# Four attentions of a decoder: exponentials of turned scores, and sequences half a step apart

## Chip, cores and metric

The kernel runs on one core of one Trainium2 chip. The metric is the device time in microseconds (us) of that core; lower is better.

## The reference

A decoder over 16 sequences of 128 tokens, width 128, 16 heads of 8. Fifteen stages follow each other; after each sub-layer `x = layernorm(x + sublayer(x))`. Four of them are attentions of this form, with softmax over the keys in float32:

```python
def attention(x, c, Wq, bq, Wk, bk, Wv, bv, Wo, bo, mask):
    qh, kh, vh = split_heads(x @ Wq + bq), split_heads(c @ Wk + bk), split_heads(c @ Wv + bv)
    s = einsum('bhqd,bhkd->bhqk', qh, kh) / sqrt(8)
    attn = softmax(s + mask, axis=-1)
    return merge_heads(einsum('bhqk,bhkd->bhqd', attn, vh)) @ Wo + bo
```

- X0 (`S_X0`): queries from x, keys and values from a context; keys masked per sequence.
- SELF2 (`S_SELF2`): q, k and v come from MLPs, computed for all sequences by the stage before and kept in SBUF; no mask.
- X2 (`S_X2`): like X0, without a mask.
- MQA (`S_MQA`): q and k are rotated by position; causal mask.

The others are an LSTM with positional attention, an attention with a threshold (REG), a linear attention (LIN), a wide one-head attention, feed-forward layers, a latent attention (LAT) and a mixture of experts.

## The kernel before

Everything stays in SBUF: `x_all` holds the state, a stage reads and writes it sequence by sequence. Each engine has its own hand-written program, and semaphores couple them. There are two buffers, `arena[0]` and `arena[1]`, and two sets of four PSUM banks, `ps[0]` and `ps[1]`; a loop turn works on a pair of sequences, s = 0 and 1, one in each (`pairs`, `PAIRS` = 8). The attention functions `att_pe`, `att_act`, `att_dve` and `att_pool` serve the four stages above and REG and LIN. Phase by phase, for both sequences of a pair:

1. POOL copies x (and the context) to the arena; PE transposes x and makes q, k (turned: width on partitions) and v, with bias products (L496 to L504, in PSUM banks 3 and 2); ACT copies them out (L623, L626), in MQA DVE rotates q and k instead (L692, L695). In SELF2 ACT copies the kept q and v.
2. POOL widens k (L422): 128x512, in which each of four column groups keeps only one head of each row group. PE then gets the scores of four heads with one fp32 product of 32 rows and 512 columns (L521), four of them for 16 heads, each into its bank, in the order 1, 2, 3, 0. Masks are added by a bf16 product with the identity (L535). Queries lie on the partitions, keys along the free axis.
3. DVE takes the maximum of each head (L727). For banks 1 and 3 it only scales the maximum (L730) and ACT exponentiates four heads separately with it as bias (L643); for banks 2 and 0 DVE subtracts (L733) and ACT exponentiates 512 columns (L640).
4. PE transposes the weights, 16 of 128x128 (L557), back into the score banks, ACT copies them out (L648), and PE multiplies values by turned weights (L543; the values carry a column of ones, which gives the sum). ACT copies the result (L653), PE turns it back (L571), DVE divides by the sum (L747, L754).
5. PE transposes the result (L580), ACT copies it (L661), PE multiplies by the output weights (L587); DVE adds x and takes mean and variance (L380, L338, L340, L343), POOL takes the power -1/2 (L332), DVE normalises (L347).

In the loop body the projections of the next pair are issued before phase 5, and widening k of its second sequence stands behind the norm's power on POOL. Tile names: `ps` is PSUM, `C` the constants (`ident` is the identity), `WA` and `WB` weights, `R` rows of gains and biases. The profile gives the line of the helper, L314 for a bias product (`add_bias`), L332 to L347 for the norm. An fp32 product is two MATMUL records with two LDWEIGHTS, a transpose or a bf16 product one. The latent stage, to which the prediction refers, is another function: there DVE scales maxima (L2044) while POOL scales weights (L1827).

## Time and profile before

| | us |
|---|---|
| median of 3 runs | 2589.38 (2586.69 to 2591.61) |
| profiled execution | 2588.07 |
| its span | 2586.3 |

| engine | busy us | share | instructions |
|---|---|---|---|
| PE, matmul | 1804.1 | 70% | 13203 |
| PE, weight load | 1172.2 | 45% | 13225 |
| DVE (VectorE) | 1442.6 | 56% | 4308 |
| ACT (ScalarE) | 1170.4 | 45% | 3283 |
| POOL (GpSimd) | 583.3 | 23% | 910 |

The profiled execution took 2588.07 us, of which the span of the records is 2586.3. The four attentions lie at 310 to 483 us (X0), 1165 to 1322 (SELF2), 1322 to 1500 (X2) and 1697 to 1881 (MQA). The mean granted TensorE clock is 0.877 of full speed over the span. The ends of matmuls in the records are modelled, so PE's busy share is no share of its peak. The profile slices the span in 40 parts of 64.7 us.

### The profile page before, as it was taken

The page shows a single profiled execution, that of the slowest core. Times are in us where ns is not written, and L with a number is a line of the kernel's source. Part 1 is how long each engine was busy: PE and PEld are TensorE (multiplying, and loading weights), DVE is VectorE, ACT ScalarE, POOL GpSimd, SP SyncE. Part 2 cuts the span into 40 slices and gives each one's busy share as a digit, 9 for nine tenths or more (in the row PEclk, how much of TensorE's full clock was granted, in tenths as well). Part 3 has the DMA queues.
Part 4 walks back from the last instruction along what each step waited for, and adds up shares of the span by engine and source line. Part 5 has one row for each costly group of instructions (what it writes and reads, how often), then busy time and mean ns, then how long its engine had stood idle before and what let it go on. Part 6 is the DMA issues. An engine that isn't in the chain of part 4 may idle for free.

```text
span 2586.3 us, 43908 instructions
## 1 busy us (share of the span) xinstructions
PE 1804.1 (70%) x13203; PEld 1172.2 (45%) x13225; DVE 1442.6 (56%) x4308; ACT 1170.4 (45%) x3283; POOL 583.3 (23%) x910
## 2 busy tenths in 40 slices
PE   2444488677755565797778821178878999998798
PEld 1333244344433353454445410144466777776343
DVE  3322555556667656316655567756655444453677
ACT  1222466456611132237756621146646655555343
POOL 2500411111122232101111133321133333333110
PEclk9999999799967687798888855589989999999899
DMA  5000000000000000000020000000000000000000
GB/s 179 1 0 0 0 0 0 0 1 0 0 1 0 0 0 0 0 0 0 0 84 0 0 1 0 0 1 0 0 1 0 0 0 0 0 0 1 1 0 16
DMA packets 2924, 18.74 MB, mean 7 GB/s; under 512 B 1073, under 2 KB 1201, under 8 KB 1585
## 3 DMA queue, kind: packets, MB, share of 16 engines
q1 hardware_dynamic: 2866, 18.02, 1.9%
q8 instruction: 30, 0.49, 0.1%
q14 instruction: 28, 0.23, 0.0%
HBM read 16.90 MB, written 1.05 MB: 7 GB/s over the span
## 4 chain that ended last, share of the span: by engine, by line
issue 53%; PE 18%; POOL 13%; POOLq 5%; ACT 5%; DVE 4%; DVEq 2%; ACTq 0%
POOL arena L1827 5%; PE ps L2195 4%; POOL arena L332 4%; POOL arena L422 3%; PE ps L521 3%; PE ps L1722 2%; ACT arena L648 1%; PE ps L535 1%; DVEq L728 1%; PE ps L314 1%; PE ps L1733 1%; ACT arena L643 1%; ACT arena L640 1%; POOLq L1515 1%; POOL arena L1499 1%
## 5 line engine op out<-in xcount | busy, mean ns | idle before, releaser
L332 POOL TENSOR_TENSOR arena<-arena,C 128x1 f32<-128x1 f32 (+1 forms) x272 | 158.0, 583 | 741.8 <-DVE arena L343 736.8
L557 PE MATMUL ps<-C,arena 128*128 128x128 f32 x1280 | 212.5, 306 | 76.6 <-ACT arena L643 64.2
L643 ACT ACTIVATE arena<-ps,arena 128x128 f32<-128x128 f32 x640 | 186.5, 394 | 172.2 <-DVE arena L730 172.2
L521 PE MATMUL ps<-arena 32*128 32x512 f32 x768 | 164.7, 769 | 108.1 <-POOL arena L422 107.4
L422 POOL TENSOR_TENSOR arena<-arena,C 128x512 f32<-128x512 f32 x96 | 99.9, 1041 | 602.3 <-ACT arena L623 303.4
L727 DVE TENSOR_REDUCE arena<-ps 128x4 f32<-128x512 f32 x320 | 219.2, 685 | 20.1 <-PE ps L535 10.0
L557 PEld LDWEIGHTS ps<-C,arena 128*128 128x128 f32 x1280 | 148.5, 152 | 160.6 <-ACT arena L643 123.9
L1827 POOL TENSOR_TENSOR arena<-arena 128x512 f32<-128x512 f32 x128 | 133.7, 1045 | 248.9 <-DVE arena L2050 245.7
L648 ACT COPY arena<-ps 128x512 f32<-128x512 f32 x320 | 166.5, 643 | 0.0
L543 PE MATMUL ps<-arena 128*32 128x128 f32 x3072 | 154.6, 305 | 7.9 <-DVE arena L717 0.9
L1055 PE MATMUL ps<-hid,WA 128*20 128x16 f32 x1024 | 57.3, 197 | 119.2 <-DVE hid L1115 114.3
L1978 ACT ACTIVATE arena<-ps,arena 128x256 f32<-128x256 f32 x256 | 119.3, 471 | 33.5 <-DVE arena L2044 21.4
L2195 PE MATMUL ps<-WA,arena 128*128 128x512 f32 x256 | 132.7, 600 | 0.9 <-ACT arena L2219 0.4
L521 PEld LDWEIGHTS ps<-arena 32*128 32x128 f32 x768 | 50.3, 214 | 170.2 <-issue 141.6
L1894 PE MATMUL ps<-arena 128*128 128x256 f32 x512 | 120.2, 386 | 0.2
L347 DVE TENSOR_SCALAR x_all<-arena 128x128 f32 x192 | 96.8, 504 | 41.4 <-POOL arena L332 40.9
L733 DVE TENSOR_TENSOR arena<-ps,arena 128x512 f32<-128x512 f32 x160 | 110.7, 692 | 12.9 <-issue 1.5
L2042 DVE TENSOR_REDUCE arena<-ps 128x2 f32<-128x512 f32 x128 | 87.7, 685 | 51.5 <-PE ps L1894 51.5
L380 DVE TENSOR_TENSOR arena<-ps,x_all 128x128 f32<-128x128 f32 x112 | 32.6, 291 | 150.2 <-PE ps L314 79.8
L1531 PE MATMUL ps<-C,arena 128*128 128x128 f32 x32 | 13.1, 461 | 147.7 <-DVE arena L1624 108.1
L640 ACT ACTIVATE arena<-arena 128x512 f32<-128x512 f32 x160 | 106.4, 665 | 19.9 <-DVE arena L733 19.9
L1904 PE MATMUL ps<-C,arena 128*128 128x128 f32 x512 | 86.2, 310 | 41.5 <-POOL arena L1827 40.9
(364 smaller groups left out, 4048.1 us busy)
## 6 DMA issues: line engine op xcount, KB each, us to landing
WA<-w_late SPq DMA_DIRECT2D x1, 4228.0 KB, 13.1
R<-rows SPq DMA_DIRECT2D x1, 2114.0 KB, 10.8
WA<-w_early SPq DMA_DIRECT2D x1, 1600.0 KB, 24.9
WB<-w_rest SPq DMA_DIRECT2D x1, 1152.0 KB, 18.2
xT_all<-x_T SPq DMA_DIRECT2D x1, 1024.0 KB, 6.2
...
```

What stands on the lines that cost most here:

```text
L332: nc.gpsimd.tensor_tensor(v_(s, cols, "rstd", 0, n), v_(s, cols, "mv", 1, 2 * n - 1)[:, ::2] if n > 1 else v_(s, cols, "mv", 1, 1), cst("m ...
L422: return eng.tensor_tensor(heads(v_(s, ATT, "wide", 0, 512)), src.unsqueeze(1).broadcast_to([128, 4, 128]), cst("tilemask").unsqueeze(2).b ...
L521: mm = nc.tensor.matmul(ps[s][t][:, :], v_(s, ATT, "kT" if kind == "linear" else "qT")[rows, :], v_(s, ATT, "wide", 0, 512)[rows, :], star ...
L543: mm = nc.tensor.matmul(ps[s][1][PAD * j:PAD * (j + 1), t * 128:(t + 1) * 128], va[:, 4 * t + j, :], v_(s, ATT, "PT", 128 * (4 * t + j), 128),
L557: mm = nc.tensor.transpose(ps[s][t][:, j * 128:(j + 1) * 128], v_(s, ATT, "P", 128 * (4 * t + j), 128), ident)
L640: nc.scalar.activation(e, e, ACT.Exp, scale=SCALE).then_inc(p_exp, 1)
L643: ex = nc.scalar.activation(e[:, 128 * j:128 * j + 128], ps[s][t][:, 128 * j:128 * j + 128], ACT.Exp, scale=SCALE, bias=v_(s, ATT, "m", 4 ...
L648: nc.scalar.copy(v_(s, ATT, "PT", 512 * t, 512), ps[s][t][:, :]).then_inc(pT_sb, 1)
L727: nc.vector.tensor_reduce(m[:, 4 * t:4 * t + 4], heads(ps[s][t][:, :]), AXX, ALU.max)
L1827: nc.gpsimd.tensor_tensor(p, p, rec.unsqueeze(2).broadcast_to([128, 2, 256]), ALU.mult).then_inc(l_sub, 1)
L1894: mm = nc.tensor.matmul(ps[s][t][:, 256 * (h % 2):256 * (h % 2) + 256], v_(s, LAT, "qT", 128 * h, 128), kT[:, 4 * hf + t, :], start=True, ...
L2195: nc.tensor.matmul(o, v_(s, MOE, "xT"), WA[:, W_LATE("experts", FF * e, FF)], start=True, stop=False, skip_group_check=True)
```

## The change

X0, SELF2, X2 and MQA get functions of their own (`satt_pool`, `satt_pe`, `satt_act`, `satt_dve`); REG and LIN keep the old ones. Two things change.

**Turned scores.** The scores are computed twice. The first time as before, with masks, for the maxima of each query (`scores`, `maxima`). The second time turned, keys on partitions and queries along the free axis: the widened operand is now q, the other k (`scores_T`), and masks are added turned (`mask_T`). A maximum belongs to a query, which is now a column, so it can't be a bias. DVE cuts the 16 maxima of each query into a bf16 part and a bf16 rest (`m_cols`), PE transposes them by a product with the identity, DVE multiplies them with a mask of -1 into a bf16 operand (`FOLD`), and PE adds this with a product with ones (`fold_T`). ACT then exponentiates 512 columns four times out of PSUM straight into the place of turned weights. The transposes of the weights and their copies are gone. POOL widens k and q.

**Half a step apart.** A turn of the loop still holds two sequences, but as two steps, one after the other (`in_turn`, `step`). In the step of sequence n, PE also issues the scores of n+1, the projections of n+2 and the output product of n-1; DVE also takes the maxima of n+1 and the norm of n-1.

Core of the diff (call sites, semaphores and declarations left out; `z` is the other buffer):

```diff
+        WIDE_Q, OT, FOLD, TURN = 0, 512, 1024, 1280
+
+        T_ORDER = (2, 3, 0, 1)
+        def satt_pool(pool, sub, kind):
...
+            def wides(i, s, d):
+                pool.wait_ge(qk_sb, nth(a, i, s + d))
+                if sub == S_X0:
+                    nc.gpsimd.tensor_copy(m_mask[s][:, :], x_at(maskadd, i, s + d)).then_inc(mask_sb, 1)
+                widen(nc.gpsimd, s, "wide", "kT").then_inc(k_wide, 1)
+                widen(nc.gpsimd, s, "P", "qT").then_inc(q_wide, 1)
+            def step(i, s, before=True, after=True, ahead=True):
+                if ahead:
+                    stage(i, s, 2)
+                if before:
+                    finish(i, s)
+                if ahead:
+                    wides(i, s, 2)
...
+        def satt_pe(pe, sub, kind, W, name, bias_name, mask_kind, out_w=384, out_name=None):
...
+            def scores_T(s, t):
+                nc.tensor.matmul(ps[s][t][:, :], v_(s, ATT, "kT")[rows(t), :],
+                                 v_(s, ATT, "P", WIDE_Q, 512)[rows(t), :], start=True, stop=False,
+                                 skip_group_check=True)
+            def fold_T(s, t, stop):
+                fold = v_(s, ATT, "P", FOLD, 256).bitcast(BF16)
+                return nc.tensor.matmul(ps[s][t][:, :], ones_b[rows(t), :], fold[rows(t), :], start=False, stop=stop,
+                                        skip_group_check=True)
+            def step(i, s, before=True, after=True, ahead=True):
+                pe.wait_ge(s_max, nth(st, i, s))
+                pe.wait_ge(q_wide, nth(st, i, s))
+                for t in T_ORDER[0:3]:
+                    scores_T(s, t)
+                if before:
+                    turned(i, s)
+                pe.wait_ge(m_cut, nth(st, i, s))
+                nc.tensor.matmul(ps[s][1][:, 0:128], m_cols[s][:, :], ident_b[:, :], start=True,
+                                 stop=True, skip_group_check=True).then_inc(mT_ps, 1)
+                if mask_kind is not None:
+                    for t in T_ORDER[0:3]:
+                        mask_T(s, t, False)
+                if before:
+                    output(i, s)
+                pe.wait_ge(m_fold, nth(st, i, s))
+                for t in T_ORDER[0:3]:
+                    fold_T(s, t, True).then_inc(sT_ps, 1)
+                scores_T(s, 1)
+                mm = fold_T(s, 1, mask_kind is None)
+                if mask_kind is not None:
+                    mm = mask_T(s, 1, True)
+                mm.then_inc(sT_ps, 1)
+                if after:
+                    scores(i, s, 1)
...
+                for n, t in enumerate(T_ORDER):
+                    pe.wait_ge(pT_sb, nth(a, i, s, GROUPS, n + 1))
...
+                mm.then_inc(oT_ps, 1)
+                if ahead:
+                    front_x(i, s, 2)
+                pe.wait_ge(oT_sb, nth(a, i, s))
...
+                mm.then_inc(o_ps, 1)
+                if ahead:
+                    front_qkv(i, s, 2)
...
+        def satt_act(act, sub, kind):
...
+            def step(i, s, before=True, after=True, ahead=True):
+                if before:
+                    turned(i, s)
+                for n, t in enumerate(T_ORDER):
+                    act.wait_ge(sT_ps, nth(st, i, s, GROUPS, n + 1))
+                    nc.scalar.activation(v_(s, ATT, "PT", 512 * t, 512), ps[s][t][:, :], ACT.Exp,
+                                         scale=SCALE).then_inc(pT_sb, 1)
+                act.wait_ge(oT_ps, nth(a, i, s))
+                nc.scalar.copy(v_(s, ATT, "P", OT, 512), ps[s][2][:, :]).then_inc(oT_sb, 1)
+                if ahead:
+                    front_x(i, s, 2)
+                    front_qkv(i, s, 2)
...
+        def satt_dve(dve, sub, kind):
...
+            def step(i, s, before=True, after=True, ahead=True):
+                m = heads(v_(s, ATT, "m"))
+                cut = m_cols[s][:, :].rearrange("p (t c) -> p t c", c=PAD)
+                dve.drain()
+                nc.vector.tensor_copy(cut[:, :, 0:4], m)
+                dve.drain()
+                nc.vector.tensor_tensor(cut[:, :, 4:8], m, cut[:, :, 0:4], ALU.subtract).then_inc(m_cut, 1)
+                dve.wait_ge(mT_ps, nth(st, i, s))
+                nc.vector.tensor_tensor(heads(v_(s, ATT, "P", FOLD, 256).bitcast(BF16)),
+                                        ps[s][1][:, 0:128].unsqueeze(1).broadcast_to([128, 4, 128]),
+                                        cst("foldmask").unsqueeze(2).broadcast_to([128, 4, 128]),
+                                        ALU.mult).then_inc(m_fold, 1)
+                if before:
+                    moments(i, s)
+                if after:
+                    maxima(i, s, 1, 0, 2)
+                if before:
+                    normed(i, s)
+                if after:
+                    maxima(i, s, 1, 2, 4)
+                dve.wait_ge(o_ps, nth(a, i, s))
...
+                if ahead and sub == S_MQA:
+                    rope(i, s, 2)
```

How the order moves on PE in X2, in the last pair, which has no next one. Before, with the scores of both sequences ahead of it (`ps0` and `ps1` are the banks of the two sequences, L521 scores, L557 transposes of weights, L543 values, L571 turning back):

```order
L557 MATMUL ps0_1<-C,arena0 128x128 x4
L557 MATMUL ps0_2<-C,arena0 128x128 x4
L557 MATMUL ps0_3<-C,arena0 128x128 x4
L557 MATMUL ps0_0<-C,arena0 128x128 x4
L543 MATMUL ps0_1<-arena0 32x128 x16
L557 MATMUL ps1_1<-C,arena1 128x128 x4
L557 MATMUL ps1_2<-C,arena1 128x128 x4
L557 MATMUL ps1_3<-C,arena1 128x128 x4
L557 MATMUL ps1_0<-C,arena1 128x128 x4
L543 MATMUL ps1_1<-arena1 32x128 x16
L571 MATMUL ps0_0<-C,arena0 128x128 x4
L571 MATMUL ps1_0<-C,arena1 128x128 x4
```

Now, in one step of the loop, sequence 1 (L913 turned scores, L931 the result of sequence 0, L950 the maxima, L937 and L326 the output of sequence 0, L925 folds, L900 scores of the next sequence, L973 values):

```order
L913 MATMUL ps1_2<-arena1 128x512
L913 MATMUL ps1_3<-arena1 128x512
L913 MATMUL ps1_0<-arena1 128x512
L931 MATMUL ps0_2<-C,arena0 128x128
L950 MATMUL ps1_1<-ident_b,m_cols1 128x128
L937 MATMUL ps0_3<-WB,arena0 128x128
L326 MATMUL ps0_3<-bias3,ones_b 128x128
L925 MATMUL ps1_2<-arena1,ones_b 128x512
L925 MATMUL ps1_3<-arena1,ones_b 128x512
L925 MATMUL ps1_0<-arena1,ones_b 128x512
L913 MATMUL ps1_1<-arena1 128x512
L925 MATMUL ps1_1<-arena1,ones_b 128x512
```

```order
L900 MATMUL ps0_1<-arena0 128x512
L900 MATMUL ps0_2<-arena0 128x512
L900 MATMUL ps0_3<-arena0 128x512
L900 MATMUL ps0_0<-arena0 128x512
L973 MATMUL ps1_2<-arena1 32x128 x16
L867 MATMUL ps1_0<-C,arena1 128x128
L981 MATMUL ps1_3<-C,arena1 128x128 x4
```

The scores of the next sequence now stand between the last turned product and the values, and the output product of the sequence before stands ahead of the folds.

DVE in MQA, before, at the end of a pair (L747 and L754 divide by the sums, L692 and L695 rotate):

```order
L747 RECIPROCAL arena0<-ps0_0 128x16
L754 TENSOR_TENSOR arena0<-ps0_0,arena0 128x128
L739 REGISTER_ALU
L747 RECIPROCAL arena1<-ps1_0 128x16
L754 TENSOR_TENSOR arena1<-ps1_0,arena1 128x128
L689 ISA
L692 TENSOR_TENSOR arena0<-ps0_3,C 128x256 x2
L695 TENSOR_TENSOR arena0<-arena0 128x256
L689 REGISTER_ALU
L692 TENSOR_TENSOR arena1<-ps1_3,C 128x256 x2
L695 TENSOR_TENSOR arena1<-arena1 128x256
```

Now, at the end of the step of sequence 0 and the begin of that of 1 (L1102 and L1104 divide, L1052 and L1055 rotate, L1083 and L1085 cut the maxima, L1087 folds, L1070 begins the norm of the sequence before, L1062 takes maxima):

```order
L1102 RECIPROCAL arena0<-ps0_3 128x16
L1104 TENSOR_TENSOR arena0<-ps0_3,arena0 128x128
L1052 TENSOR_TENSOR arena0<-ps0_1,C 128x256 x2
L1055 TENSOR_TENSOR arena0<-arena0 128x256
L1083 CAST m_cols1<-arena1 128x4x4
L1085 TENSOR_TENSOR m_cols1<-arena1,m_cols1 128x4x4
L1087 TENSOR_TENSOR arena1<-ps1_1,C 128x512
L1070 TENSOR_TENSOR arena0<-ps0_3,x_all 128x128
L350 BN_STATS arena0<-arena0 128x6
L352 BN_AGGR arena0<-arena0 128x2
L355 TENSOR_SCALAR arena0<-arena0 128x1
L1062 TENSOR_REDUCE arena0<-ps0_1 128x4
```

The rotation of the sequence two further on now stands ahead of cutting the maxima of the next.

POOL in SELF2, in the loop now (L435 widens k, then q; L344 is the power of the norm):

```order
L343 ISA
L344 TENSOR_TENSOR arena1<-arena1,C 128x1
L836 REGISTER_ALU
L435 TENSOR_TENSOR arena0<-arena0,C 128x512 x2
L343 REGISTER_ALU
L344 TENSOR_TENSOR arena0<-arena0,C 128x1
L836 REGISTER_ALU
L435 TENSOR_TENSOR arena1<-arena1,C 128x512 x2
L811 REGISTER_ALU
L811 COMPARE_AND_BRANCH
```

Each step now has two widenings in one go, where it had one.

## Rows read from the trace of the kernel before

**Rows 1.** Windows: stretch, length, busy PE, PEld, DVE, ACT, POOL, clock, DMA.

```profile
310.00:483.00 173.00, 143.93 (x1247) 81.97 (x1247) 99.30 (x240) 108.34 (x304) 32.77 (x62) 0.99 0.00 0
...
329.84:478.33 148.49, 124.65 (x1091) 70.38 (x1090) 87.61 (x211) 94.05 (x264) 28.28 (x52) 0.99 0.00 0
...
1180.29:1317.19 136.90, 108.71 (x899) 61.56 (x897) 88.06 (x211) 97.81 (x256) 22.11 (x28) 0.86 0.00 0
...
1342.79:1492.44 149.65, 121.79 (x1035) 74.92 (x1034) 87.61 (x210) 94.05 (x264) 28.28 (x52) 0.87 0.00 0
...
1717.74:1875.74 158.00, 132.44 (x1175) 79.05 (x1174) 104.13 (x253) 97.09 (x256) 25.44 (x40) 1.00 0.00 0
```

**Rows 2.** Timeline, one pair of X2: start, length, engine, line, idle before.

```profile
1436.15 1.23 PE L521 MATMUL ps<-arena 32*128 32x512 f32 x8 [1.97 <-POOL arena L422]
...
1438.17 2.00 PE L557 MATMUL ps<-C,arena 128*128 128x128 f32 x8 [0.79 <-ACT arena L643]
...
1449.55 0.26 DVE L747 RECIPROCAL arena<-ps 128x16 f32<-128x16 f32 x1 [4.50 <-PE ps L571]
...
1449.88 0.29 DVE L754 TENSOR_TENSOR arena<-ps,arena 128x128 f32<-128x128 f32 x1
```

**Rows 3.** The page, granted TensorE clock in 40 slices, tenths of full.

```profile
PEclk9999999799967687798888855589989999999899
```

**Rows 4.** Groups by line and form: busy us, mean ns of one, idle before.

```profile
L727 DVE TENSOR_REDUCE arena<-ps 128x4 f32<-128x512 f32 x320 | 219.2, 685 | 20.1 <-PE ps L535 10.0 <-PE ps L521 9.6 <-issue 0.3
...
L557 PE MATMUL ps<-C,arena 128*128 128x128 f32 x1280 | 212.5, 306 | 76.6 <-ACT arena L643 64.2 <-ACT arena L640 11.5
...
L733 DVE TENSOR_TENSOR arena<-ps,arena 128x512 f32<-128x512 f32 x160 | 110.7, 692 | 12.9 <-issue 1.5
...
L640 ACT ACTIVATE arena<-arena 128x512 f32<-128x512 f32 x160 | 106.4, 665 | 19.9 <-DVE arena L733 19.9
...
L422 POOL TENSOR_TENSOR arena<-arena,C 128x512 f32<-128x512 f32 x96 | 99.9, 1041 | 602.3 <-ACT arena L623 303.4 <-DVE arena L695 102.6 <-PE ps L571 95.6
...
L535 PE MATMUL ps<-causal_b,ident_b 128*128 128x512 bf16 x64 | 16.6, 382 | 0.0
```

**Rows 5.** Timeline, where work runs back to back, in SELF2, X2 and MQA.

```profile
1269.48 2.03 ACT L648 COPY arena<-ps 128x512 f32<-128x512 f32 x4
...
1270.54 1.45 PE L543 MATMUL ps<-arena 128*32 128x128 f32 x32
...
1428.54 0.39 PE L496 MATMUL ps<-arena,WB 128*128 128x128 f32 x2
...
1429.49 0.44 PE L496 MATMUL ps<-arena,WB 128*128 128x128 f32 x2
...
1448.91 1.16 PE L571 MATMUL ps<-C,arena 128*128 128x128 f32 x8
...
1811.28 0.75 DVE L692 TENSOR_TENSOR arena<-ps,C 128x256 f32<-128x256 f32 x2 [0.41 <-PE ps L499]
...
1812.11 0.43 DVE L695 TENSOR_TENSOR arena<-arena 128x256 f32<-128x256 f32 x1
...
1816.98 1.23 PE L521 MATMUL ps<-arena 32*128 32x512 f32 x8 [0.90 <-POOL arena L422]
...
1818.14 1.04 PE L535 MATMUL ps<-causal_b,ident_b 128*128 128x512 bf16 x4
```

**Rows 6.** Timeline, small DVE operations and POOL, X2, then the latent stage.

```profile
1434.26 0.34 DVE L347 TENSOR_SCALAR x_all<-arena 128x128 f32 x1
...
1435.04 1.05 DVE L347 TENSOR_SCALAR x_all<-arena 128x128 f32 x1 [0.44 <-POOL arena L332]
...
2099.99 1.04 POOL L1827 TENSOR_TENSOR arena<-arena 128x512 f32<-128x512 f32 x1 [0.17 <-DVE arena L2050]
...
2100.61 0.45 DVE L2044 TENSOR_SCALAR arena<-arena 128x2 f32<-128x2 f32 x1
...
2101.72 0.17 DVE L2044 TENSOR_SCALAR arena<-arena 128x2 f32<-128x2 f32 x1
```

More of the change, by code:

```diff
@@ L450, in wide @@
                     pool.wait_ge(o_ps, nth(a, i, s))
-                widen(nc.gpsimd, i, d, s, kind).then_inc(wide_ok, 1)
+                widen(nc.gpsimd, s, "wide", "qT" if kind == "linear" else "kT").then_inc(wide_ok, 1)
             def body(i, ahead):
@@ L792, in att_dve, with in_turn, stage, finish @@
             pairs(dve, front, body)
+        def in_turn(eng, step, last):
+            step(0, 0, before=False)
+            step(0, 1)
+            with eng.Fori(1, PAIRS - 1) as i:
+                step(i, 0)
+                step(i, 1)
+            step(PAIRS - 1, 0, ahead=False)
+            step(PAIRS - 1, 1, ahead=False, after=False)
+            last(PAIRS - 1, 2)
+        def satt_pool(pool, sub, kind):
+            a, st = att_run[sub], st_run[sub]
+            def stage(i, s, d):
+                if d == 0:
+                    pool.wait_ge(seq_done, nth(sub, i, s))
+                elif kind == "cross":
+                    pool.wait_ge(qkv_ps, nth(qkv_run[sub], i, s, 2, 2))
+                elif kind == "self":
+                    pool.wait_ge(xT_ps, nth(xt_run[sub], i, s))
+                if kind == "cross":
+                    nc.gpsimd.tensor_copy(v_(s, ATT, "c"), x_at(ctxT_all, i, s + d))
+                if kind != "kept":
+                    nc.gpsimd.tensor_copy(v_(s, ATT, "x"), x_at(x_all, i, s + d))
+                    pool.drain()
+                pool.sem_inc(staged, 1)
+            def wides(i, s, d):
[4 more added lines that the diff above has]
+                widen(nc.gpsimd, s, "P", "qT").then_inc(q_wide, 1)
+            def finish(i, s):
+                rstd(pool, var_ok, rstd_ok, tail_run[sub], i, (s + 1) % 2, ATT, 1, s - 1 - (s + 1) % 2)
+            def step(i, s, before=True, after=True, ahead=True):
[5 more added lines that the diff above has]
+                    wides(i, s, 2)
+            for s in range(2):
+                stage(0, s, 0)
+            for s in range(2):
+                wides(0, s, 0)
+            in_turn(pool, step, finish)
@@ new lines, in satt_dve, with rope, maxima, moments @@
+        def satt_dve(dve, sub, kind):
+            a, st = att_run[sub], st_run[sub]
+            def rope(i, s, d):
+                dve.wait_ge(qkv_ps, nth(qkv_run[sub], i, s + d, 2, 1))
+                qk, turn = qkT_of(s), v_(s, ATT, "P", TURN, 256)
+                for dst, at, table in ((qk, 0, "cos"), (turn, 256, "sin")):
+                    nc.vector.tensor_tensor(heads(dst, 2), heads(ps[s][1][:, at:at + 256], 2),
+                                            cst(table).unsqueeze(1).broadcast_to([128, 2, 128]), ALU.mult)
+                dve.drain()
+                nc.vector.tensor_tensor(qk, qk, turn, ALU.add).then_inc(qk_sb, 1)
+            def maxima(i, s, d, of, to):
+                z = (s + d) % 2
+                for n in range(of, to):
+                    t = ORDER[n]
+                    dve.wait_ge(s_ps, nth(a, i, s + d, GROUPS, n + 1))
+                    red = nc.vector.tensor_reduce(v_(z, ATT, "m", 4 * t, 4), heads(ps[z][t][:, :]), AXX, ALU.max)
+                if to == GROUPS:
+                    red.then_inc(s_max, 1)
+            def moments(i, s):
+                z = (s + 1) % 2
+                r = v_(z, ATT, "r")
+                dve.wait_ge(y_ps, nth(tail_run[sub], i, s - 1))
+                nc.vector.tensor_tensor(r, ps[z][3][:, 0:128], x_at(x_all, i, s - 1), ALU.add).then_inc(y_read, 1)
+                dve.drain()
+                stats(dve, z, ATT, r).then_inc(var_ok, 1)
+            def normed(i, s):
+                z = (s + 1) % 2
+                dve.wait_ge(rstd_ok, nth(tail_run[sub], i, s - 1))
+                norm(dve, z, ATT, x_at(x_all, i, s - 1), v_(z, ATT, "r")).then_inc(seq_done, 1)
+            def step(i, s, before=True, after=True, ahead=True):
+                m = heads(v_(s, ATT, "m"))
+                cut = m_cols[s][:, :].rearrange("p (t c) -> p t c", c=PAD)
+                dve.drain()
+                nc.vector.tensor_copy(cut[:, :, 0:4], m)
+                dve.drain()
+                nc.vector.tensor_tensor(cut[:, :, 4:8], m, cut[:, :, 0:4], ALU.subtract).then_inc(m_cut, 1)
[13 more added lines that the diff above has]
+                dve.wait_ge(o_ps, nth(a, i, s))
+                o = ps[s][3][:, :].rearrange("p (h d) -> p h d", d=PAD)
+                rec = v_(s, ATT, "rec")
+                nc.vector.reciprocal(rec, o[:, :, HD:HD + 1].rearrange("p h d -> p (h d)"))
+                dve.drain()
+                nc.vector.tensor_tensor(v_(s, ATT, "O").rearrange("p (h d) -> p h d", d=HD), o[:, :, 0:HD],
+                                        rec.unsqueeze(2).broadcast_to([128, HEADS, HD]), ALU.mult).then_inc(o_sb, 1)
+                if ahead and sub == S_MQA:
+                    rope(i, s, 2)
+            def last(i, s):
+                moments(i, s)
+                normed(i, s)
+            if sub == S_MQA:
+                for s in range(2):
+                    rope(0, s, 0)
+            maxima(0, 0, 0, 0, 4)
+            in_turn(dve, step, last)
@@ L928, in start_dve @@
             nc.vector.memset(minus_round[:, :], -ROUND)
+            for s in range(2):
+                nc.vector.memset(m_cols[s][:, :], 0.0)
             dve.wait_ge(bias_in, 16)
```

174 lines of the change are left out of this document (148 added, 26 removed).

## Prediction

> **What bounds the kernel now.** I read the stretches first: what does a pair of sequences take in each of the four attentions? Between the first and the last pair, seven pairs take 148.49 us in X0, 136.90 in SELF2, 149.65 in X2 and 158.00 in MQA [rows 1], so a pair takes 21.21, 19.56, 21.38 and 22.57 us, and a sequence 10.61, 9.78, 10.69 and 11.29: 42.36 together, and 16 sequences of each 677.8 us. All of X0 is 173.0 us [rows 1], 3.3 more than eight pairs. No engine is full in them: in X2 PE is busy 121.8 of 149.65 us, DVE 87.6, ACT 94.1. So the order of the work bounds, not a count. The reader sees it next in the timeline of one pair of X2 [rows 2]: all engines do the same phase for both sequences, then hand over. PE stands 1.97 us before the second group of scores, for the widened keys of POOL, which stand behind the norm; DVE stands 4.50 us before the reciprocal, while ACT copies turned weights and PE multiplies; ACT waits out the maxima. The granted clock shows it too [rows 1, 3]: 0.99 in X0 and 1.00 in MQA, but 0.86 and 0.87 in SELF2 and X2, where after the wait of 1.97 us eight transposes take 2.00 us [rows 2].
>
> **What goes.** Per sequence 16 PE transposes of weights (L557), four ACT copies of them (four in 2.03 us) and 2 DVE subtractions (692 ns); eight short ACT exponentials become two wide ones [rows 4, 5]. What comes: four turned score products and four folded maxima on PE (and four more masks where there are any), a transpose of the maxima, one DVE fold, two small DVE operations, a second POOL widening. PE's total hardly moves: 212.5 us over 80 sequences [rows 4], 2.7 each, go; 2.6 come by the prices below. DVE is about even, ACT loses 2 us or more of its 6.7 (94.05 / 14). The gain is to come from the stagger: ACT's four exponentials of sequence n now lie beside PE's scores of n+1 and DVE's maxima of n+1, and the tail of n-1 in the gaps.
>
> **The new period.** One sequence per period; I follow the loop from the end of DVE's fold.
>
> *A, PE from the folds to the weights times values.* Four row-tiled fp32 score products take 1.23 us with their tail, the masks start 1.16 after them; four masks take 1.04, one alone 382 ns, so 0.22 apart and 0.16 of tail [rows 4, 5]. Three folds: side by side in separate rows 0.3, one after another 0.65; I take 0.5, and 0.2 for the last. The turned product left alone: no row shows one. At least a quarter of a group, 0.3; at most what a whole group takes, 1.16; being alone it has nothing to share its stream with, so 0.9. Next scores 1.2. Values: after ACT's last copy (1269.48 + 2.03 = 1271.51) PE ended at 1271.99 [rows 5]; less hand-over and tail a quarter is 0.25, so 1.0. Without masks 0.5 + 0.9 + 0.2 + 1.2 + 1.0 = **3.8**; with masks 0.2 and 0.9 more, **4.9**. Covered: ACT's exponentials, 0.35 + 4 x 0.55 = 2.55 (L640's 0.665 is one with its latency, the copies came 0.5 apart), against 2.8 of PE ahead of the values; DVE's norm of n-1 and its four maxima (0.685 each [rows 4]), done just before the sums are. If PE's part shrank, those maxima would set the end next.
>
> *B.* Tail, ACT's copy of the sums 0.65, two hand-overs: 0.9. Then four transposes, half of the eight in 1.16: 0.5 [rows 5]. Together **1.4**.
>
> *C, until the small maxima operations are done.* X0 and X2: PE issues the three projections of n+2, 0.95 (L496 at 1428.54 and 1429.49 [rows 5]), three turned products 0.9 and a transpose 0.15: **2.0**. DVE takes 1.3 beside it: hand-over 0.1, the product 0.33 behind the reciprocal [rows 2] and 0.29 long, cast and subtraction 0.5 with their drains (0.17 is what a 128x2 operation takes [rows 6]). SELF2 has no projections, so DVE's 1.35 would set it. MQA must rotate: DVE needs four of its five projections, 4/3 of 0.95 or 1.3, 0.2 of tail and hand-over, then 0.75 + 0.43 + 0.1 [rows 5] and 0.5 for the small ones: 3.3.
>
> Here a lock counts. In the latent stage DVE's tensor_scalar on 128x2 takes 0.17 us alone and 0.45 when POOL's tensor_tensor runs: it ends with that one, at 2101.06 against 2101.03. The norm at 1435.04 takes 1.05 instead of 0.34, under a widening [rows 6]. So even tiny operations between places in SBUF wait for POOL's running instruction. The change issues two widenings of 1.04 us [rows 4] per sequence as soon as q and k lie ready: in SELF2 while DVE does the reciprocal, so the cast or the subtraction waits for the rest of the second, +1.0; in MQA in the same instant as the cast, so the subtraction waits for the first, +0.7. In X0 and X2 q and k are ready 1.3 us after the projections begin, when both are just over: 0. Bounds: 0 and 2.1. So SELF2 **2.35**, MQA **4.0**. The Trainium skill says the same more widely ("SBUF — State Buffer", Who interferes with whom): a DVE cast, or one with two SBUF inputs, is fully blocked by a GpSimd instruction that reads SBUF. By that rule the cast and the subtraction both count, and the fold, with one input in PSUM, doesn't; the rows above agree for a tensor_scalar, and for a subtraction no row here shows it.
>
> *D.* The maxima's transpose and hand-overs 0.35, DVE's fold 0.7 (L733, 692 ns, the nearest [rows 4]) and 0.05: **1.1**. PE's output and masks (1.0) fit beside it.
>
> Sum: X0 4.9 + 1.4 + 2.0 + 1.1 = **9.4**; X2 **8.3**; SELF2 3.8 + 1.4 + 2.35 + 1.1 = **8.65**; MQA **11.4**. Together 37.75, times 16 is 604: 74 us less than 677.8. MQA gains nothing; its rotation and the small operations lie end to end. The ends cost more: before, X0 had 3.3 us beside its pairs. Now the first sequence waits for its scores and maxima alone (1.2 + 2.4) while the last steps are short; I take 3 a stage, 12 (bounds 0 and 6). ACT's table load (1.28 us a pair in SELF2 and MQA) falls between the copy of the outputs and the first exponential, where ACT waits. POOL's rstd comes before DVE has done two maxima. So 62 us less: 2588.07 (span 2586.3) becomes **2526 us**. The median of the runs, 2589.38, lies 1.3 from the profiled one.
>
> **The clock.** I take it full in all four. Before, it was low after the wait of 1.97 us in X2; MQA waits 0.90 at that place [rows 5] and keeps 1.00. The longest PE wait in the sum is SELF2's, 1.4.
>
> **Rivals.**
> 1. *No lock on the small operations.* The 128x2 operation is a tensor_scalar; a cast to bf16 of 4x4 may run free. SELF2 -1.0, MQA -0.7, times 16: -27, **2499 us**. Against it speak the 0.45 and 1.05 us [rows 6]. Chance 0.13.
> 2. *The clock stays where it was*, 0.86 in SELF2 and X2. PE paces 4.5 us of SELF2's period (A, the transposes, little else) and 6.9 of X2's (A, transposes, C, the start of D). At 0.86 to 0.87 they take 0.155 more: 11.4 x 0.155 x 16 = +28, **2554 us**. For it: both stages keep several short waits in each period. Against: the long one goes. Chance 0.17.
> 3. *The lock takes both small operations.* If POOL starts a moment ahead of the cast, the cast waits for the first widening and the subtraction for the second: +1.3 in MQA, +0.5 in SELF2, times 16: +29, **2555 us**. Chance 0.10.
> 4. *Slower: the clock falls to its lower level.* A stage with several PE waits each period can lose the full clock: the feed-forward stage behind X2 has 5 and 5 in its slices [rows 3]. Where SELF2 and X2 ran at 0.5 throughout, +182: **2708 us**. The point from which it is no gain is 182 x (1/c - 1) = 62, c = 0.75 in these two (or 0.87 in all four, where PE paces some 27 us of the 37.75). For it speak SELF2's 0.86 before and its lock; against it, that no wait is as long as before. Chance 0.05.
> 5. *The turned products do not run side by side*, 0.9 each: three are 2.7. +1.8 in X0 and X2, +0.5 in SELF2: +66, **2592 us**, no change. L521's groups of four in 1.16 us, fp32 and row-tiled alike, speak against it. Chance 0.02.
>
> My forecast has 0.53. **Range**: down to rival 1 with the lone product and folds cheaper (16 us), 2485; up to rival 2 or 3 and some 20 us of a dearer lone product or ends, 2575. Outside remain the fifth and fourth, and the tails. Faster by over 0.2% (5 us, about what a measurement here can tell from no change): 0.92. Within: 0.02. Slower: 0.06.
>
> **What would show it.** Product starts (DVE's x rec) 9.4, 8.65, 8.3, 11.4 us apart in X0, SELF2, X2, MQA. In SELF2 and MQA a cast or subtraction of 0.5 to 1.2 us that ends with a widening; in X0 and X2 at 0.2. ACT idle before the first exponential, not after. PE's longest wait for the maxima's cast in SELF2 and MQA, for ACT's copy of the sums in X0 and X2. PEclk 0.95 or more in all four. It is wrong if the periods are right but the clock isn't, if PE waits for exponentials before the values, or if a lone turned product takes 0.4 or 2 us.

## Result, and the profile after

| | before | after |
|---|---|---|
| median, us | 2589.38 | 2606.34 (2602.17 to 2608.71, 5 runs) |
| profiled execution, us | 2588.07 | 2608.71 |
| its span, us | 2586.3 | 2606.8 |
| mean granted clock | 0.877 | 0.847 |
| ratio of times | | 1.0064, interval 1.0053 to 1.0075 |

The changed kernel is slower by 0.6%; 2526 us was forecast. Busy times and the granted clock in 40 slices, from the page of the kernel after (the clock line answers to [rows 3]):

```profile
PE 1861.7 (71%) x13161; PEld 1155.5 (44%) x13161; DVE 1417.9 (54%) x4246; ACT 961.7 (37%) x2631; POOL 647.4 (25%) x990
...
PEclk9999999699967777886669755688789999998899
```

ACT lost 209 us of work and the kernel gained no time by it. PE has 42 fewer matmuls, but 57.6 us more busy time. Counted from 0, slices 18 to 20 (SELF2) and 26 to 29 (MQA) show where its clock went.

Windows of the kernel after (stretch, length, busy PE, PEld, DVE, ACT, POOL, clock, DMA), against [rows 1]: first X0 as a whole; then each stage from the start of the first sequence's product (x rec) to that of the last; then pieces of SELF2 and MQA:

```profile
310.00:471.50 161.50, 146.86 (x1265) 74.37 (x1264) 86.06 (x225) 58.99 (x144) 54.24 (x95) 0.97 0.00 1
...
328.80:465.08 136.28, 128.64 (x1159) 65.31 (x1157) 76.78 (x206) 54.31 (x131) 46.43 (x83) 1.00 0.00 0
1168.63:1319.22 150.59, 132.21 (x907) 64.02 (x904) 81.30 (x206) 51.47 (x116) 35.58 (x42) 0.64 0.00 0
1344.26:1462.20 117.94, 106.03 (x1045) 60.30 (x1043) 84.17 (x206) 54.38 (x131) 42.86 (x69) 0.99 0.00 1
1684.34:1896.05 211.71, 178.23 (x1243) 84.24 (x1241) 115.81 (x249) 50.74 (x117) 39.74 (x56) 0.81 0.00 0
1189.99:1205.27 15.28, 11.93 (x125) 6.13 (x127) 11.14 (x29) 6.84 (x16) 5.17 (x7) 1.00 0.01 1
1227.51:1262.03 34.52, 31.66 (x186) 15.08 (x186) 16.78 (x42) 10.58 (x24) 7.75 (x10) 0.50 0.00 0
1684.34:1696.28 11.94, 9.65 (x87) 5.17 (x86) 8.07 (x18) 3.35 (x8) 2.82 (x4) 1.00 0.01 1
```

Each piece holds whole sequences: two of SELF2 at 1.00 take 15.28 us, 7.64 each; three at 0.50 take 34.52, 11.51 each. One of MQA at 1.00 takes 11.94; others there take up to 16.8. X0 and X2 keep a steady period, 9.26 and 7.82 us, at full clock.

By stage, between the same operations in both traces (ACT's first copy of SELF2 at 1163.96 and 1152.00, the norm that ends it at 1322.06 and 1323.52, and so on): X0 12.0 us less, SELF2 13.4 more, X2 32.4 less, MQA 49.8 more, the rest 1.7 more; together the 20.5 us of the spans.

Timeline of the kernel after (start, length, engine, line, idle before in brackets): the fill of SELF2, a sequence of SELF2 at 1.00, one at 0.50, one of X2 at full clock, one of MQA on its way down:

```profile
1153.58 1.14 PE L900 MATMUL ps<-arena 32*128 32x512 f32 x8 [2.58 <-POOL arena L435]
...
1157.27 1.23 PE L913 MATMUL ps<-arena 32*128 32x512 f32 x3 [2.56 <-DVE arena L1062]
...
1161.00 1.57 ACT L1031 ACTIVATE arena<-ps 128x512 f32<-128x512 f32 x3 [6.59 <-PE ps L925]
...
1196.65 2.04 POOL L435 TENSOR_TENSOR arena<-arena,C 128x512 f32<-128x512 f32 x2 [2.61 <-ACT arena L1011]
...
1198.08 0.64 DVE L1083 CAST m_cols<-arena 128x16 bf16<-128x16 f32 x1 [0.16 <-issue]
...
1238.58 2.09 PE L913 MATMUL ps<-arena 32*128 32x512 f32 x6
...
1249.04 1.11 PE L981 MATMUL ps<-C,arena 128*128 128x128 f32 x4 [0.71 <-ACT arena L1034]
...
1375.74 0.66 PE L981 MATMUL ps<-C,arena 128*128 128x128 f32 x4 [0.45 <-ACT arena L1034]
...
1377.27 1.13 PE L913 MATMUL ps<-arena 32*128 32x512 f32 x6
...
1377.67 0.90 DVE L1085 TENSOR_TENSOR m_cols<-arena,m_cols 128x16 bf16<-128x16 f32 x1
...
1378.34 0.33 PE L931 MATMUL ps<-C,arena 128*128 128x128 f32 x1
...
1378.89 0.69 DVE L1087 TENSOR_TENSOR arena<-ps,C 128x512 bf16<-128x512 f32 x1 [0.32 <-PE ps L950]
...
1379.64 0.39 PE L925 MATMUL ps<-arena,ones_b 32*128 32x512 bf16 x3
...
1379.64 1.12 PE L913 MATMUL ps<-arena 32*128 32x512 f32 x2
...
1381.77 1.08 PE L973 MATMUL ps<-arena 128*32 128x128 f32 x32
...
1383.56 0.66 PE L981 MATMUL ps<-C,arena 128*128 128x128 f32 x4 [0.45 <-ACT arena L1034]
...
1740.73 2.04 POOL L435 TENSOR_TENSOR arena<-arena,C 128x512 f32<-128x512 f32 x2 [9.89 <-DVE arena L1055]
1740.74 1.06 DVE L1083 CAST m_cols<-arena 128x16 bf16<-128x16 f32 x1
...
1741.88 0.92 DVE L1085 TENSOR_TENSOR m_cols<-arena,m_cols 128x16 bf16<-128x16 f32 x1
...
1742.86 0.29 PE L950 MATMUL ps<-ident_b,m_cols 128*128 128x128 bf16 x1 [1.84 <-DVE m_cols L1085]
...
1742.93 1.49 PE L919 MATMUL ps<-ident_b,causal_b 128*128 128x512 bf16 x3
```

In MQA both widenings start with the cast; the cast ends with the first and the subtraction (0.17 us free) with the second; PE waits 1.84 us, and its masks then take 1.49 us for three, where [rows 5] has four in 1.04. In SELF2 at 0.50 PE hardly waits at all: the longest gap of the sequence at 1238 is 0.71, but six records of turned scores take 2.09 us against 1.13 at full clock. Its long waits lie ahead of the steady part, in the fill: 2.58 us before the first scores and 2.56 us before the first turned scores. There the clock falls (windows of 5 us, same columns as above):

```profile
1150.00:1155.00 5.00, 2.14 (x17) 1.08 (x16) 1.02 (x3) 2.39 (x5) 2.52 (x3) 1.00 0.01 2
1155.00:1160.00 5.00, 2.31 (x7) 0.61 (x7) 2.96 (x7) 0.00 (x0) 1.51 (x2) 0.55 0.00 0
1160.00:1165.00 5.00, 4.63 (x26) 2.15 (x30) 0.70 (x2) 2.17 (x4) 0.00 (x0) 0.50 0.00 0
```

Behind the fill it does not stay put either: the distances between SELF2's products are 11.5, 9.9, 7.6, 7.6, 10.7, four of 11.5, then 9.9, 7.6, 7.6, 10.7, 11.5 and 9.8 us, so the clock comes back twice and is lost twice, with the same work in every sequence.

Groups of the kernel after (busy us, mean ns of one | idle before), beside [rows 4]:

```profile
L913 PE MATMUL ps<-arena 32*128 32x512 f32 x512 | 177.8, 755 | 12.2 <-DVE arena L1062 12.2
...
L1062 DVE TENSOR_REDUCE arena<-ps 128x4 f32<-128x512 f32 x256 | 163.9, 685 | 153.9 <-PE ps L909 88.7 <-PE ps L900 65.2
...
L1031 ACT ACTIVATE arena<-ps 128x512 f32<-128x512 f32 x256 | 134.6, 600 | 145.0 <-PE ps L925 136.4 <-PE ps L919 8.6
```

DVE and ACT now wait for PE (the maxima 153.9 us, the exponentials 145.0); before, the maxima waited 20.1 us. PE now paces the stages, so its clock is in the time: half the clock makes 11.51 us of 7.64.

### The profile page after: what moved, and what is told of

Read it like the earlier page. It is cut to its first block, busy times and chain, and to the rows that moved or that the text cites. A ratio compares the mean times of both kernels' runs of the same rounds, so it can differ in the third digit from the quotient of the medians.

```text
span 2606.8 us, 42884 instructions
## 1 busy us (share of the span) xinstructions
PE 1861.7 (71%) x13161; PEld 1155.5 (44%) x13161; DVE 1417.9 (54%) x4246; ACT 961.7 (37%) x2631; POOL 647.4 (25%) x990
## 4 chain that ended last, share of the span: by engine, by line
issue 39%; PE 36%; POOL 10%; DVE 6%; POOLq 5%; ACT 3%; DVEq 1%; ACTq 0%
POOL arena L2156 5%; PE ps L913 5%; PE ps L2524 4%; PE ps L900 3%; POOL arena L344 3%; PE ps L973 3%; PE ps L2051 2%; PE ps L981 2%; PE ps L925 1%; PE ps L880 1%; PE ps L909 1%; PE ps L326 1%; PE ps L919 1%; PE ps L534 1%; ACT arena L1034 1%
## 5 line engine op out<-in xcount | busy, mean ns | idle before, releaser
L344 POOL TENSOR_TENSOR arena<-arena,C 128x1 f32<-128x1 f32 (+1 forms) x272 | 156.6, 578 | 768.0 <-DVE arena L355 763.0
L435 POOL TENSOR_TENSOR arena<-arena,C 128x512 f32<-128x512 f32 x160 | 163.6, 1040 | 494.0 <-ACT arena L1011 156.5
L1062 DVE TENSOR_REDUCE arena<-ps 128x4 f32<-128x512 f32 x256 | 163.9, 685 | 153.9 <-PE ps L909 88.7
L1031 ACT ACTIVATE arena<-ps 128x512 f32<-128x512 f32 x256 | 134.6, 600 | 145.0 <-PE ps L925 136.4
L913 PE MATMUL ps<-arena 32*128 32x512 f32 x512 | 177.8, 755 | 12.2 <-DVE arena L1062 12.2
L1860 PE MATMUL ps<-C,arena 128*128 128x128 f32 x32 | 13.1, 460 | 147.6 <-DVE arena L1953 107.0
L900 PE MATMUL ps<-arena 32*128 32x512 f32 x512 | 116.3, 810 | 2.6 <-POOL arena L435 2.6
L2233 PE MATMUL ps<-C,arena 128*128 128x128 f32 x512 | 86.1, 310 | 41.4 <-POOL arena L2156 40.9
L350 DVE BATCH_NORM_STATS2 arena<-arena 128x6 f32<-128x128 f32 (+1 forms) x304 | 102.0, 336 | 24.3 <-POOLq L2136 2.7
L2223 PEld LDWEIGHTS ps<-arena 128*128 128x128 f32 x512 | 94.6, 190 | 24.2 <-ACT arena L2322 6.4
L326 PE MATMUL ps<-bias,ones_b 128*128 128x128 bf16 (+1 forms) x352 | 105.3, 299 | 0.0
L534 PE MATMUL ps<-arena 32*128 32x512 f32 x256 | 52.7, 879 | 64.1 <-POOL arena L435 64.0
L359 DVE TENSOR_SCALAR x_all<-arena 128x128 f32 (+1 forms) x192 | 76.9, 401 | 34.5 <-POOL arena L344 34.0
L2233 PEld LDWEIGHTS ps<-C,arena 128*128 128x128 f32 x512 | 63.8, 156 | 62.4 <-POOL arena L2156 59.9
```

The source lines that it names most:

```text
L326: return nc.tensor.matmul(out_ap, ones_b[:, :], bias3[:, BIAS(name, of, width)], start=False, stop=stop, skip_group_check=True)
L344: nc.gpsimd.tensor_tensor(v_(s, cols, "rstd", 0, n), v_(s, cols, "mv", 1, 2 * n - 1)[:, ::2] if n > 1 else v_(s, cols, "mv", 1, 1), cst("m ...
L435: return eng.tensor_tensor(heads(v_(s, ATT, dst, of, 512)), v_(s, ATT, src).unsqueeze(1).broadcast_to([128, 4, 128]), cst("tilemask").unsq ...
L900: mm = nc.tensor.matmul(ps[z][t][:, :], v_(z, ATT, "qT")[rows(t), :], v_(z, ATT, "wide", 0, 512)[rows(t), :], start=True, stop=mask_kind i ...
L913: nc.tensor.matmul(ps[s][t][:, :], v_(s, ATT, "kT")[rows(t), :], v_(s, ATT, "P", WIDE_Q, 512)[rows(t), :], start=True, stop=False, skip_gr ...
L1031: nc.scalar.activation(v_(s, ATT, "PT", 512 * t, 512), ps[s][t][:, :], ACT.Exp, scale=SCALE).then_inc(pT_sb, 1)
```

## Experiments

The theory from the trace: the change made PE the pace of all four stages, and PE's clock fell in two of them; in MQA the lock adds its own time. Rival: the waits lower the clock, and taking the lock's wait away brings it back everywhere. In the session of the first four kernels the kernel before took 2587.03 us (7 runs), in that of the last four 2590.23 us; each ratio is to the one of its session. Below, "a sequence" is the distance between two starts of the product.

### The lock taken away: `late_widen`

```diff
                 pool.wait_ge(qk_sb, nth(a, i, s + d))
+                if d:
+                    pool.wait_ge(m_cut, nth(st, i, s + 1))
```

POOL widens for sequence n+2 only once DVE has cut the maxima of n+1.

> Edit: POOL widens k and q of sequence n+2 only after DVE has cut the maxima of n+1, so no widening can meet the cast or the subtraction. Theory 'lock wait': the 1.84 us PE wait behind cast (1.06 us) and subtraction (0.92 us) is what lets the clock fall in MQA. Then the cast and subtraction are 0.17 us everywhere, MQA's period is 10.6 to 11.2 us at a clock of 0.97 or more (234 us of stage become 180), the total about 2545 to 2560 us. Rival 'the steps themselves': the clock falls without a lock, because what remains of PE's work doesn't keep it. Then MQA gains only the 1.6 us per step it waited (about 25 us), SELF2 stays near 0.6 with periods of 11 us, total 2575 to 2585 us. SELF2 tells most: its wait for the lock is only 0.5 us.

Measured: 2543.37 us (2509.80 to 2544.93, 4 runs), ratio 0.9784 (0.9716 to 0.9852). Windows of MQA from first to last sequence, and of a piece of SELF2; then the small operations by tile (lines are 2 higher than in the kernel after; min/median/max ns):

```profile
1684.19:1835.18 150.99, 140.37 (x1243) 74.31 (x1241) 92.92 (x248) 49.62 (x117) 39.75 (x56) 1.00 0.00 1
1165.00:1280.00 115.00, 105.45 (x615) 50.21 (x614) 51.99 (x138) 35.19 (x81) 25.29 (x29) 0.50 0.00 0
```

```profile
L1085 DVE CAST m_cols<-arena x64: 174/175/176, 318.6 to 1828.9; 128x16 bf16<-128x16 f32 x64
L1087 DVE TENSOR_TENSOR m_cols<-arena,m_cols x64: 174/176/177, 318.9 to 1829.2; 128x16 bf16<-128x16 f32 x64
```

The lock is gone (longest cast 176 ns, after: 1059), and MQA takes 10.3 us a sequence at 1.00 throughout, 60.7 us less between the same points. SELF2 does not follow: nine sequences of 11.5 us, one of 9.8, and only then 7.3, 7.3, 7.3 and 8.9. So the rival holds for MQA. In SELF2 the lock's wait was not what kept the clock down: PE is 105.45 us of 115.00 busy at 0.50. The fill's waits, which this edit leaves, stand ahead of it. At full clock a sequence takes 7.3 us here against 7.6 with the lock, and X2's 7.7 against 7.8; X0 keeps 9.3. One of the four executions took 2509.8 us, with no further edit.

### Work in PE's waits: `warm_full` and `warm_rows`

```diff
+            first, second = {S_SELF2: (2, 3), S_MQA: (5, 3)}.get(sub, (0, 0))
+            def warm(o, n, k):
+                for _ in range(n):
+                    nc.tensor.matmul(heads(o, k), ident_b[slice(0, 128), :],
+                                     ones_b[slice(0, 128), :].unsqueeze(1).broadcast_to([128, k, 128]), ...)
...
+                warm(ps[s][1][:, 128:512], first, 3)
                 pe.wait_ge(m_cut, nth(st, i, s))
...
+                warm(ps[s][3][:, :], second, 4)
                 pe.wait_ge(oT_sb, nth(a, i, s))
```

The lock stays. Both kernels add idle bf16 matmuls whose results nobody reads: `warm_full` over all 128 rows of the array, `warm_rows` with `slice(0, 32)` in place of `slice(0, 128)`, over 32 rows.

> Edit: the kernel after the change, with filler products on PE in SELF2 and MQA, in the places where PE waits: before the wait for the cut maxima (2 in SELF2, 5 in MQA, 384 columns each) and before the wait for ACT's copy of the sums (3 of 512 columns). They use all 128 rows of the array, bf16, into PSUM that is free there. Both theories of the clock say that it comes back when PE has work in its waits: SELF2's clock from 0.63 to 0.9 or more, its periods 7.7 to 8.3 us (stage 175 becomes 130 to 138 us); MQA 12.0 to 12.6 us per step at 0.95 or more (234 becomes 200 to 206 us). Total 2530 to 2545 us. If the fall of the clock is not the cause of the loss, the fillers only cost: 2610 us or more.

> Edit: the same fillers at the same places, same number and columns, but each with 32 rows of operands instead of 128, so PE is occupied for the same time. Theory 'waits': any occupation of PE brings the clock back, so the same as the full fillers, 2530 to 2545 us. Theory 'kind of work': the change took the 16 transposes through the whole array out and put products of 32 rows in; more of that kind doesn't bring the clock back: SELF2 stays at 0.5 to 0.65 with periods of 11 to 12 us, total 2600 to 2630 us.

Measured: `warm_full` 2539.79 us, ratio 0.9810 (0.9793 to 0.9826); `warm_rows` 2661.43 us, ratio 1.0273 (1.0252 to 1.0294). Windows from first to last sequence, SELF2 and MQA, of `warm_full`:

```profile
1169.42:1283.13 113.71, 102.20 (x982) 49.88 (x976) 80.44 (x206) 50.31 (x116) 35.31 (x42) 1.00 0.00 1
1656.21:1830.75 174.54, 159.71 (x1363) 83.77 (x1361) 115.75 (x248) 49.66 (x117) 39.84 (x56) 1.00 0.00 0
```

and the same of `warm_rows`:

```profile
1170.01:1358.50 188.49, 185.93 (x982) 79.84 (x979) 76.22 (x207) 51.86 (x116) 34.95 (x42) 0.50 0.00 0
1735.17:1960.50 225.33, 211.93 (x1363) 97.72 (x1361) 115.75 (x248) 50.81 (x117) 39.75 (x56) 0.77 0.00 0
```

Work added to the engine that sets the pace took some 66 us off the kernel (ratio 1.0064 to 0.9810). SELF2 takes 7.6 us a sequence, MQA 11.9, all at 1.00: the clock alone costs SELF2 36.9 us (150.59 to 113.71) and MQA 37.2 (211.71 to 174.54). That X2's first two sequences are 13.3 and 9.1 us here (9.3 and 7.8 in the kernel after) takes some back. The fillers of 32 rows do the opposite: PE is 185.93 of 188.49 us busy, and the clock stays at 0.50, 12.7 us a sequence. In SELF2 a PE without waits is not enough to bring the clock back; that falls with this row. `warm_rows` lies 31 us above the expected 2630: its fillers lie on the path, 12.7 us a sequence in SELF2 against 11.5 at 0.50 without them, and MQA takes 225.33 us against 211.71.

### Old functions where the clock fell: `mixed`

```diff
-                satt_pe(pe, S_SELF2, "kept", WA, None, None, None, 0, "self2_out")
+                att_pe(pe, S_SELF2, "kept", WA, None, None, None, 0, "self2_out")
-                satt_pe(pe, S_MQA, "self", WB, "mqa", "mqa", "causal")
+                att_pe(pe, S_MQA, "self", WB, "mqa", "mqa", "causal")
```

The same on ACT, DVE and POOL, with POOL widening k of SELF2 from where the old function did: the change in X0 and X2 alone.

> Edit: one part of the change alone. X0 and X2 with the new functions, SELF2 and MQA with the old ones. Every theory that puts the loss into SELF2 and MQA says: X0 161.5 and X2 143 us as in the kernel after, SELF2 157 and MQA 184 us as before. That is 11.5 + 35 us below the kernel before: 2540 to 2550 us. If the new stages hurt their neighbours (the clock carried over from stage to stage), X2 behind the old SELF2 or REG behind X0 would be slower, and the total 2560 us or more.

Measured: 2541.37 us (2539.34 to 2543.29), ratio 0.9818 (0.9801 to 0.9834). X2 takes 7.8 us a sequence, SELF2 and MQA 19.5 and 22.6 a pair, as before. The change is worth 46 us in two of the stages, and in the other two it gave back 63 (13.4 and 49.8 by stage).

### Both together: `late_fill_self2`, `late_fill_sum`, `late_burst`

The later widening, and in SELF2 alone five fillers a sequence; two; or twelve once, in the fill of the stage, behind its first scores:

```diff
+            first, second = {S_SELF2: (2, 3)}.get(sub, (0, 0))
...
+            first, second = {S_SELF2: (0, 2)}.get(sub, (0, 0))
...
+            if sub == S_SELF2:
+                for _ in range(12):
+                    nc.tensor.matmul(heads(ps[1][3][:, :]), ident_b[:, :], ...)
```

> The later widening of late_widen, and in self-attention 2 alone two and three full-array bfloat16 matmuls of idle data per sequence where PE waits for the cut scores and for the sums copy. If that stage's 11.5 us a sequence in late_widen were only the lower clock (two steps at 1.00 took 7.6 us each, three at 0.50 took 11.5 us each): 7.3 to 7.7 us a sequence over the whole stage, MQA unchanged at 10.3, a granted clock above 0.87, and 2543 less about 9 x 4 = 2500 to 2510 us. If the fillers' own time (five of them, about 0.2 us each at full clock) stands on the path: 8.5 us a sequence and about 2515 to 2525 us. If the clock falls for another reason than what PE does in its waits: no gain, 2540 to 2560 us.

> The later widening, and only two full-array matmuls per sequence of self-attention 2, in the wait for the sums copy (none in the wait for the cut scores). If a little full-array work is enough at any place: as late_fill_self2, 2495 to 2510 us with 7.3 to 7.6 us a sequence. If both waits must be filled: the stage is at 11.5 us a sequence for most of its length, 2535 to 2550 us.

> The later widening, and twelve full-array matmuls of 512 columns once, ahead of the first sequence of self-attention 2. If that stage keeps whichever clock level it starts with (late_widen showed nine sequences of 11.5 us and then only 7.3 us): 7.3 to 7.7 us from the first sequence to the last and 2500 to 2515 us. If the pattern of a sequence pulls the clock down again: the first one or two sequences at 7.6, then 11.5, and 2535 to 2550 us, as late_widen.

Measured: `late_fill_self2` 2507.89 us, ratio 0.9688 (0.9674 to 0.9702), SELF2 at 7.6 us a sequence. `late_fill_sum` 2504.50 us (2503.32 to 2511.37), ratio 0.9676 (0.9660 to 0.9693). Windows of its SELF2, X2 and MQA, each from the second sequence to the last:

```profile
1174.10:1275.37 101.27, 88.24 (x874) 43.23 (x874) 69.93 (x192) 46.88 (x108) 34.15 (x40) 1.00 0.00 0
1312.60:1421.05 108.45, 96.50 (x974) 56.03 (x972) 69.86 (x192) 50.69 (x122) 39.75 (x64) 0.99 0.00 0
1654.40:1795.09 140.69, 130.73 (x1158) 69.13 (x1157) 86.52 (x231) 46.32 (x109) 36.94 (x52) 1.00 0.00 1
```

SELF2 takes 7.3 us a sequence, X2 7.7 after two slow ones (13.3 and 8.8), MQA 10.3. It is faster than both kernels, 3.2% below the one before. Two fillers in the wait for the sums do; three more only cost 0.3 us a sequence. `late_burst`: 2514.52 us (2501.76 to 2523.18), ratio 0.9720 (0.9694 to 0.9746). Its profiled execution took 2501.76 us. Here are its products in the fill, the clock of that fill, and all of SELF2 from the first sequence to the last:

```profile
1152.38 2.76 PE L1000 MATMUL ps<-ones_b,ident_b 128*128 128x512 bf16 x12
...
1155.00:1160.00 5.00, 4.21 (x50) 2.10 (x53) 1.65 (x4) 2.07 (x4) 0.00 (x0) 1.00 0.00 0
...
1162.12:1273.88 111.76, 89.74 (x907) 46.22 (x905) 75.07 (x206) 50.52 (x116) 36.73 (x43) 0.97 0.00 1
```

SELF2 takes 7.3 us a sequence but for two of 8.9. The twelve products stand in the second wait of the fill, where the clock of the kernel after fell to 0.55, and the clock stays at 1.00. The same sequences that ran at 0.50 in `late_widen` run near full clock once PE has not lost it ahead of them. So it is in the fill's waits that SELF2 first loses the clock, and the work of its sequences does not soon bring it back. The full clock doesn't always hold, as the 21 us between its executions show; where they lost it, no trace shows.

### Full clock for the kernel before: `before_fill`

```diff
+                    if s == 1 and sub in (S_SELF2, S_X2):
+                        for _ in range(8):
+                            nc.tensor.matmul(heads(ps[1][1][:, :]), ident_b[:, :], ...)
```

> The kernel before, with eight full-array matmuls of 512 columns per pair of sequences in self-attention 2 and cross-attention 2, ahead of the second sequence's scores, where PE waits 1.97 us. It tells how much of any gain the fillers bring without the change. If the clock of these stages (0.86 before) is all they touch, and the stages are bound by other engines' waits: 2575 to 2595 us. If PE at full clock would shorten the old stages as well: each of two stages loses up to its 14 per cent of PE's share, 2560 to 2575 us. If the fillers stand on the path: eight of 0.21 us less the 1.97 us wait, nothing to 10 us more, up to 2600 us.

Measured: 2589.52 us (10 runs), ratio 1.0000 (0.9991 to 1.0010). SELF2 and X2, same stretches as in [rows 1]:

```profile
1180.17:1317.19 137.02, 111.70 (x955) 58.53 (x953) 88.20 (x211) 97.82 (x256) 22.06 (x28) 0.98 0.00 0
1342.74:1492.43 149.69, 125.31 (x1091) 72.78 (x1090) 87.63 (x211) 94.04 (x264) 28.21 (x52) 0.98 0.00 0
```

The clock goes from 0.86 and 0.87 to 0.98, and seven pairs take 137.02 and 149.69 us where they took 136.90 and 149.65. The old order has so much slack on PE that its clock costs nothing there. None of the gain of the kernels above is a gain that the old one could have had from fillers in these two stages.

## Why the prediction was wrong

**The step that failed** is the clock: "I take it full in all four." It was 0.64 in SELF2 and 0.81 in MQA. `warm_full`, which is the changed kernel with a full clock in these two, took 2539.79 us, 14 above the forecast and inside its range; the clock is the 66 us that carry the result over to the other side. My reason was the length of PE's waits: "the longest PE wait in the sum is SELF2's, 1.4", and that "no wait is as long as before". That was so in the steady sequences of SELF2, whose longest waits are 0.7 us. But the sum left out two kinds of wait. In the fill of SELF2, PE waits 2.58 and 2.56 us, more than the 1.97 of before, and the clock goes from 1.00 to 0.50 there; with twelve products in the second of them, in `late_burst`, it stays at 1.00. In MQA the lock makes PE wait up to 1.84 us a sequence; with that wait gone, in `late_widen`, the clock is 1.00 throughout.

And I had nothing on how the clock comes back. In SELF2, PE has no projections: what is left is mostly products of 32 rows or 32 columns, and in `late_widen` nine sequences of them ran at 0.50 with PE almost full. X0 and X2, which have projections, kept the clock. That full-array products bring it back and 32-row products don't is shown (`warm_full`, `warm_rows`); that projections do the same in X0 and X2 is not. SELF2's 0.86 before [rows 1] was a hint of it that I laid to a wait alone. `before_fill` doesn't tell the two apart: its eight full-array products stand in that wait, and they brought 0.98.

The Trainium skill ("TensorE: Matmul & The Clock Gate", HAM oscillation) names gaps between matmuls as what takes the clock down. The 1.84 us of MQA and their cure in `late_widen` agree, and so do SELF2's fill and `late_burst`; the 0.50 of `warm_rows`, with 2.6 us of gaps in 188.49, does not, and there the measurement decides.

**The periods at full clock**, point by point, in X2: DVE's fold ended at 1379.58 and the values at 1382.85, A = 3.27 (3.8 forecast); to the end of the turning, 1384.22, B = 1.37 (1.4); from the turning before, 1376.40, to the end of the subtraction, 1378.57, C = 2.17 (2.0); to the end of the fold, D = 1.01 (1.1). Together 7.82 against 8.3. X0 has 9.26 against 9.4. The lone turned product took no more than 0.97 (1379.64 to the last fold's product at 1380.61): 0.9 was right. Three turned products, six records, took 1.13 us and three folds 0.39, so both run side by side. That excludes rival 5.

**The lock.** The mechanism was right, the size was not. MQA: +0.7 forecast for one blocked operation; both were blocked, and the difference between 11.94 (`warm_full`) and 10.3 us (`late_widen`), both at 1.00, is 1.6 a sequence, 26 us in all. That is the mechanism of rival 3, which had 2.0 there. The 10.3 are also less than the 11.29 of before, so without the lock MQA gains too, where I forecast that it couldn't. SELF2: +1.0 forecast; the widenings start while DVE still takes maxima, the cast loses 0.47 us (0.64 against 0.17), and without the lock the period is 7.27 instead of 7.64, so the lock costs 0.4. X2: 0 forecast, with small operations of 0.2; the subtraction did take 0.90, but PE's last turned products and the transpose of the result ran until then (0.33 us from 1378.34), and the period without the lock is shorter by only 0.1. The Trainium skill's rule ("SBUF — State Buffer", Who interferes with whom) is that a DVE cast can, and an operation with two SBUF inputs does, contend with a POOL instruction that reads SBUF. It is borne out for both: 1.06 and 0.92 us under a widening, 0.17 in `late_widen`. The fold, with one input in PSUM, took 0.69 us under the second widening of X2, as it does alone.

**The ends** were 12 us in the sum and cost about 42. In X0, 16 periods are 148.2 of 161.5 us, so 13.3 lie beside them, where before it was 3.3 [rows 1]. The first product comes 18.8 us after the stage begins, for one sequence; before, the pair had its own after 19.8. I counted only scores and maxima of the first sequence (3.6) and left out that all its other phases run with nothing beside them: in SELF2 ACT idles 6.59 us ahead of the first exponential. The lower clock of the fill is part of this. In `late_fill_sum` 16 periods are shorter by 21, 40, 48 and 16 us in the four stages, 125 together, and the span by 82.8: 42 us of ends, of which 7 are X2's two slow sequences.

**The sum again**: with the measured periods at full clock, 16 x (9.26 + 7.64 + 7.82 + 11.94) = 587 us, 91 less than 677.8, and 42 for the ends, 2588 becomes 2539; `warm_full` took 2539.79. Against the forecast the periods are 17 us better and the ends 30 us worse, 13 in all; the rest of the miss of 80 us is the clock.

**The rivals.** Rival 4 named the right mechanism, the lower level of the clock, with the wrong second stage: SELF2, yes, X2 no, and MQA instead, where the lock's wait did it. Its price was near: 4.5 us for a sequence of SELF2 at half the clock, 3.9 measured (11.51 less 7.64). Its chance of 0.05 was too low; the doubt was one sentence long, though the feed-forward row, with three slices of 5 where I wrote two, stood beside it. Rival 2 priced PE's clock of 0.86 at 28 us, with PE as pace; `before_fill` shows that before the change the same clock cost nothing, so it is the change that makes the clock count. Whether the stagger or the turned scores do, no run separates: neither half ran alone. Rival 1, no lock on the small operations, is excluded by their 1.06 and 0.92 us.
